# Attention 1: PE does the value products of two steps together in every second step

## The chip, the cores and the metric

The kernel runs on one core of a Trainium2 chip. The metric is the device time of one execution in microseconds (us), and the time shown is the median of several executions. PE is TensorE (PEld is its weight load), DVE is VectorE, ACT is ScalarE, POOL is GpSimd and SP is the queue that starts most DMAs.

## What is computed

The program is eight blocks in a row on an input of 2 x 1024 tokens with 128 features. The change touches only the first, a causal attention with 16 heads whose keys and values are made from a shared 32-wide latent. Cut to what matters, the reference is:

```
q      = einsum('bld,dhk->blhk', x, Wq)
latent = einsum('bld,dc->blc', x, Wkv_down)
k, v   = einsum('blc,chk->blhk', latent, Wk_up), einsum('blc,chk->blhk', latent, Wv_up)
attn   = softmax(where(causal, einsum('bqhd,bkhd->bhqk', q, k) / sqrt(64), -inf))
y      = einsum('bhqk,bkhd->bqhd', attn, v)
out    = einsum('bqhd,hdo->bqo', y, Wout)
```

The other seven blocks (a state-space layer, two spiking layers, two more attentions and two mixtures of experts) are written apart and are not changed.

## The kernel before

**Steps.** The attention is worked off in 96 steps, `STEPS` (t = 0 to 95). A group of four heads of one batch entry (`gg`, 8 of them) takes twelve steps: four for its first 512 queries (`c` = 0, key blocks `n` = 0 to 3) and eight for its last 512 (`c` = 1, `n` = 0 to 7). A step handles one block of 128 keys against up to 512 queries, for four heads. `width(t)` is how many queries are left under the causal mask: 512, 384, 256 and 128 for the last four blocks of either half. Below, the steps of one group are named by their numbers, and group 5, which is steps 60 to 71, stands for the others.

**What PE does in a step.** `scores(t, j)` is one matmul for each head (L532, plus the mask as a second matmul at L535 on diagonal blocks), in up to four slots that share three PSUM banks. A slot waits until ACT has taken the exponential (L695) of the slot three before it. `values(t)` multiplies the latent tokens with the exponentials of the four heads: four matmuls of 32 output columns (L548), each kept by the trace as two records, so eight records for one step. It needs all exponentials of step t. It writes bank 6 or 7. Below, V61 means `values(61)`.

**Items.** Between them PE works on a list of items, `PLAN[t]`, that prepares the next group: full score tiles for the row maxima (L581) and diagonal ones (L573 with the mask at L576), the projection of the queries (`mm3`, L46 to L48), the transposed maxima "n" (L587), the denominators "z" (L599, and L604 for late blocks) and, for a finished batch entry, the output projection "y" (L612). Items have three banks of their own. PE may begin item i only when DVE has worked off item i - 3 (the wait on `s0_af`); DVE needs one reduction for each score tile (L813, L825). An item "n" waits for the last maxima of DVE; its result goes through ACT (L711), DVE (L789) and a DMA before the scores of two steps later may start (`s0_nd`). An item "z" goes through ACT (L715, L716) and DVE (L794, L799).

**Order.** PE runs the program in the order in which it is written, and so do ACT, DVE and POOL. In step t it is: two score slots, the first third of the items, `values(t - 1)`, the second third, the other two score slots, the last third. So there is one value product in each step, one step behind its scores. POOL adds up the exponentials of the early blocks (L755); ACT may overwrite a tile of exponentials four steps later, once its value product is done (`s0_pv`) and POOL has added it (`s0_zp`). For the last half group (steps 88 to 95) PE makes the sums itself, right after the value products (L554).

Of the kernel before, what the change touches and what calls it, by code (L numbers as in the profile page):

```python
# [24 lines left out]
def wait(eng, sem, n):  # L25

    if n > 0:
        eng.wait_ge(sem, n)
# [26 lines left out]
def build(nc, a, out, upto=8):  # L55

    ctx = ExitStack()
    with ctx:
# [8 lines left out]
        def bank(i, n=1):  # L67
            return ps[:, i:i + n, :].rearrange("p b c -> p (b c)")
# [310 lines left out]
        N_STEP = len(STEPS)  # L379
        LAST = {2 * gg + c: 12 * gg + (3 if c == 0 else 11) for gg in range(NG0) for c in range(2)}  # L380

        def width(t):

            gg, c, n = STEPS[t]
            c0 = P * max(0, n - 4 * c)
            return c0, 512 - c0

        def slots(t):

            w = width(t)[1]  # L390
            return [(h, 1) for h in range(4)] if w > 256 else ([(0, 2), (2, 2)] if w == 256 else [(0, 4)])
# [51 lines left out]
        def parts(t):  # L443

            x = PLAN[t]
            if len(x) == 1 and x[0][0] == "n":
                return [], [], x
            k = (len(x) + 2) // 3
            return x[:k], x[k:2 * k], x[2 * k:]
# [35 lines left out]
        def s0_pe(pe):  # L485
# [37 lines left out]
            def scores(t, j):  # L523
                gg, c, n = STEPS[t]
                c0, w = width(t)
                h0, nh_ = slots(t)[j]
                e = SLOT_OF[t] + j
                if n == 0:
                    pe.wait_ge(s0_nd, 32 * (2 * gg + c + 1))
                wait(pe, s0_e, e - 2)  # L530
                o = bank(3 + e % 3)[:, 0:nh_ * w].rearrange("p (h q) -> p h q", h=nh_)
                ins = pe.matmul(o, kst[:, gg // G0, P * n:P * n + P], qst[gg % 2][:, c, h0:h0 + nh_, c0:512],  # L532
                                start=True, stop=True)
                if n >= 4 * c:
                    ins = pe.matmul(o[:, :, 0:P], ident_bf[:, :], causalT_bf.unsqueeze(1).to_broadcast([P, nh_, P]),  # L535
                                    start=False, stop=True, skip_group_check=True)
                ins.then_inc(s0_s, 1)

            def values(t):
                gg, c, n = STEPS[t]  # L540
                c0, w = width(t)
                u = 2 * gg + c
                src = zacc[u % 2] if n == 0 else pt[t % 4]
                pe.wait_ge(s0_e, SLOT_OF[t + 1])
                if n == 0:
                    wait(pe, s0_oc, u - 1)
                for h in range(4):
                    ins = pe.matmul(bank(6 + u % 2)[LD * h:LD * h + LD, c0:512], lat_tok[:, LB * (gg // G0) + n, :],  # L548
                                    src[:, h, 0:w], start=n == 0, stop=n == 4 * c + 3, skip_group_check=True)
                if (gg, c) == PE_SUMS:  # L550
                    i = AT[("z", u)]
                    wait(pe, s0_af, i - 2)
                    for h in range(4):
                        ins = pe.matmul(bank(i % 3)[LD * h:LD * h + LD, c0:512], ones32, src[:, h, 0:w],  # L554
                                        start=n == 0, stop=n == 4 * c + 3, skip_group_check=True)
                ins.then_inc(s0_pv, 1)
# [69 lines left out]
            for t in range(N_STEP + 2):  # L626
                first, second, third = parts(t)
                own = range(len(slots(t))) if t < N_STEP else []
                for j in own[:2]:
                    scores(t, j)  # L630
                for x in first:
                    item(x)
                if 0 < t <= N_STEP:
                    values(t - 1)
                for x in second:
                    item(x)
                for j in own[2:]:
                    scores(t, j)
                for x in third:
                    item(x)  # L640
# [2078 lines left out]
        def s6_dve(dve, link, s):  # L2719
# [40 lines left out]
            dve.reciprocal(w6i[:, (NTI - 1) % 2, :], z6[:, (NTI - 1) % 2, :]).then_inc(s6_wi_end, 1)  # L2760

        PE = {0: s0_pe, 1: s1_pe, 2: s2_pe, 3: s34_pe, 5: moe_pe, 6: s6_pe, 7: moe_pe}
        ACTS = {0: s0_act, 1: s1_act, 2: s2_act, 3: s34_act, 5: moe_act, 6: s6_act, 7: moe_act}
        DVE = {0: s0_dve, 1: s1_dve, 2: s2_dve, 3: s34_dve, 5: moe_dve, 6: s6_dve, 7: moe_dve}
# [99 lines left out]
```

## Time and profile before

| | |
|---|---|
| median of 3 runs | 2025.33 us (2019.01 to 2029.76) |
| the profiled execution | 2027.12 us, its span 2025.3 us |
| PE busy over the span | 1784.8 us, 88% |
| DVE, ACT, POOL busy | 79%, 59%, 47% |
| the 96 steps | about 67 to 434 us of the span |
| one group of 12 steps (V60 to V72) | 309.38 to 353.76 us, 44.38 us |

All numbers are times from the start of the profiled span or durations, in us unless ns is said. In rows of the timeline the first number is when a group of like instructions starts, the second how long it lasts in all, xN how many there are, and the bracket how long the engine had been idle and what ended that. The end of a matmul is modelled and its start is not, so distances between starts are read. A busy PE in this view is therefore not a PE at its peak.

### The profile page before, as it was taken

The page shows a single profiled execution, that of the slowest core. Times are in us where ns is not written, and L with a number is a line of the kernel's source. Part 1 is how long each engine was busy: PE and PEld are TensorE (multiplying, and loading weights), DVE is VectorE, ACT ScalarE, POOL GpSimd, SP SyncE. Part 2 cuts the span into 40 slices and gives each one's busy share as a digit, 9 for nine tenths or more (in the row PEclk, how much of TensorE's full clock was granted, in tenths as well). Part 3 has the DMA queues.
Part 4 walks back from the last instruction along what each step waited for, and adds up shares of the span by engine and source line. Part 5 has one row for each costly group of instructions (what it writes and reads, how often), then busy time and mean ns, then how long its engine had stood idle before and what let it go on. Part 6 is the DMA issues. An engine that isn't in the chain of part 4 may idle for free.

```text
span 2025.3 us, 33172 instructions
## 1 busy us (share of the span) xinstructions
PE 1784.8 (88%) x12499; PEld 1215.2 (60%) x12499; DVE 1596.5 (79%) x2099; ACT 1192.3 (59%) x2056; POOL 955.7 (47%) x386
## 2 busy tenths in 40 slices
PE   6899999887798987799999888889887777899999
PEld 5444454446455656677887555555555555678887
DVE  4566656528698988678876899999999999887777
ACT  2355444533697843446655667767777766655554
POOL 3266655612197951010000288878889889600000
PEclk9799999989799988799999999999999999999999
DMA  3111112000122220101100000000001000111000
GB/s 89 33 33 33 33 33 50 16 12 1 45 84 94 94 68 1 35 28 37 32 16 1 1 2 2 1 1 2 2 1 33 1 2 1 33 32 32 17 16 22
DMA packets 39555, 53.98 MB, mean 27 GB/s; under 512 B 6179, under 2 KB 22790, under 8 KB 39398
## 3 DMA queue, kind: packets, MB, share of 16 engines
q1 hardware_dynamic: 38870, 50.82, 9.0%
q8 instruction: 101, 1.65, 0.3%
q10 hardware_dynamic: 528, 1.05, 0.2%
q14 instruction: 56, 0.46, 0.1%
HBM read 37.83 MB, written 1.18 MB: 19 GB/s over the span
## 4 chain that ended last, share of the span: by engine, by line
PE 54%; issue 18%; DVE 18%; POOL 5%; ACT 3%; DMA 1%; SPq 0%; DVEq 0%; ACTq 0%; POOLq 0%; PEldq 0%
PE ps L46 10%; PE ps L47 9%; PE ps L48 9%; DVE negm L2724 7%; PE ps L1697 3%; PE ps L532 3%; PE ps L548 3%; PE ps L581 2%; PE ps L573 2%; DVE AF L2731 2%; PE ps L1685 2%; PE ps L2636 1%; POOL AR_plain L2529 1%; PE ps L2553 1%; DVE AF L825 1%
## 5 line engine op out<-in xcount | busy, mean ns | idle before, releaser
L2724 DVE TENSOR_REDUCE negm<-ps 128x64 bf16<-128x1024 f32 x256 | 301.8, 1213 | 20.1 <-PE ps L2627 20.0
L2529 POOL TENSOR_TENSOR AR_plain<-AF 128x2048 f32<-128x2048 f32 x64 | 261.7, 4094 | 31.5 <-ACT AF L2680 31.3
L46 PE MATMUL ps<-XH,AR 128*128 128x512 f32 x616 | 255.9, 415 | 23.4 <-DVE XL L251 5.9
L2688 ACT ACTIVATE AF<-ps 128x1024 f32<-128x1024 f32 x192 | 196.4, 1023 | 133.1 <-PE ps L2636 131.8
L755 POOL TENSOR_TENSOR AF<-AF 128x2048 f32<-128x2048 f32 (+3 forms) x52 | 184.7, 3551 | 179.1 <-ACT AF L695 176.2
L47 PE MATMUL ps<-XL,AR 128*128 128x512 f32 x616 | 245.5, 399 | 0.0
L48 PE MATMUL ps<-XH,AR 128*128 128x512 f32 x616 | 245.4, 398 | 0.0
L695 ACT ACTIVATE AF<-ps 128x512 f32<-128x512 f32 (+1 forms) x304 | 154.0, 576 | 147.4 <-PE ps L532 69.0
L2636 PE MATMUL ps<-negm,ident_bf 128*128 128x512 bf16 x512 | 161.3, 398 | 81.0 <-DVE negm L2724 80.6
L2731 DVE TENSOR_REDUCE AF<-AF 128x128 f32<-128x2048 f32 x96 | 218.4, 2275 | 0.0
L285 POOL TENSOR_SCALAR var_eps<-mv 128x8 f32<-128x8 f32 x10 | 4.2, 420 | 355.3 <-DVE mv L262 355.2
L1956 DVE TENSOR_TENSOR_SCAN AF<-AF,ps 128x1024 f32<-128x1024 f32 x64 | 144.4, 2275 | 18.4 <-PE ps L1685 12.8
L46 PEld LDWEIGHTS ps<-XH,AR 128*128 128x128 f32 x616 | 118.7, 193 | 66.7 <-issue 31.7
L2627 PE MATMUL ps<-AF_rounded,AR 128*128 128x256 f32 x704 | 149.5, 336 | 1.2 <-ACT AF L2688 1.1
L1335 ACT ACTIVATE AR_plain<-ps 128x512 f32<-128x512 f32 x128 | 76.5, 597 | 107.8 <-PE ps L48 107.8
L2529 POOL TENSOR_TENSOR hc<-AF 128x2048 f32<-128x2048 f32 x32 | 131.0, 4094 | 11.5 <-ACT AF L2680 11.5
L1377 DVE TENSOR_TENSOR AR_plain<-ps,AR_plain 128x512 f32<-128x512 f32 x128 | 88.1, 689 | 60.5 <-ACT AR_plain L1335 59.9
L48 PEld LDWEIGHTS ps<-XH,AR 128*128 128x128 f32 x616 | 118.9, 193 | 26.2
L47 PEld LDWEIGHTS ps<-XL,AR 128*128 128x128 f32 x616 | 119.3, 194 | 21.2
L2627 PEld LDWEIGHTS ps<-AF_rounded,AR 128*128 128x128 f32 x704 | 112.6, 198 | 31.3 <-ACT AF L2688 4.5
L2553 PE MATMUL ps<-AR_plain,AF 128*8 128x128 f32 x2752 | 113.7, 284 | 18.4 <-issue 12.3
L1335 ACT ACTIVATE AF<-ps 128x512 f32<-128x512 f32 x128 | 76.3, 596 | 87.7 <-PE ps L48 84.5
(329 smaller groups left out, 4199.2 us busy)
## 6 DMA issues: line engine op xcount, KB each, us to landing
AF<-scan_c_rows SPq DMA_DIRECT2D x32, 512.0 KB, 3.7
AR<-AR SPq DMA_DIRECT2D x96, 128.0 KB, 2.4
AF<-in_L_ffn_Wg_dram SPq DMA_DIRECT2D x21, 256.0 KB, 2.7
AF<-in_L_ffn_Wu_dram SPq DMA_DIRECT2D x21, 256.0 KB, 3.1
AF<-in_L_ffn_Wd_dram SPq DMA_DIRECT2D x21, 256.0 KB, 3.8
AF<-in_L_attn_a_Wq_dram SPq DMA_DIRECT2D x1, 512.0 KB, 4.0
AF<-in_L_attn_a_Wout_dram SPq DMA_DIRECT2D x1, 512.0 KB, 8.9
lnt<-in_L_ffn_W_fc_dram SPq DMA_DIRECT2D x2, 256.0 KB, 6.9
```

The source lines that it names most:

```text
L46: pe.matmul(out, ah, bh, start=start, stop=False)
L47: pe.matmul(out, ah, bl, start=False, stop=False)
L48: return pe.matmul(out, al, bh, start=False, stop=stop)
L695: act.activation(dst[:, h0:h0 + nh_, 0:w], bank(3 + e % 3)[:, 0:nh_ * w].rearrange("p (h q) -> p h q", h=nh_), ACT.Exp).then_inc(s0_e, 1)
L755: pool.tensor_tensor(zacc[u % 2][:, :, c0:512], zacc[u % 2][:, :, c0:512], pt[t % 4][:, :, 0:w], ALU.add).then_inc(s0_zp, 1)
L1335: act.activation(MSG[k][m % 3], bank(m % 2), ACT.Silu).then_inc(m_sg, 1)
L2529: pool.tensor_tensor(p6[m % 3].rearrange("p (j q i) -> p j q i", j=HJ, i=2), e6[m % 4].rearrange("p (j q i) -> p j q i", j=HJ, i=2), w6i[: ...
L2627: ins = pe.matmul(bank(2 * (j % 3) + x // 2)[:, 256 * (x % 2):256 * (x % 2) + 256], k6[g // LB][:, x, P * kb:P * kb + P], q[:, :, q0:q0 + ...
L2636: ins = pe.matmul(bank(2 * (j % 3) + h).rearrange("p (j q i) -> p j q i", j=4, i=2), ident_bf[:, :], negm6[:, j % 4, :].unsqueeze(1).unsqu ...
L2688: act.activation(o[:, :, q0:q0 + 2 * SUB], bank(2 * (j % 3), 2).rearrange("p (j c) -> p j c", j=HJ), ACT.Exp).then_inc(s6_e, 1)
L2724: dve.tensor_reduce(negm6[:, j % 4, :], bank(2 * (j % 3), 2).rearrange("p (j q i) -> p q j i", j=HJ, i=2), mybir.AxisListType.XY, ALU.max, ...
L2731: dve.tensor_reduce(z6[:, m % 2, :], e6[m % 4].rearrange("p (j q i) -> p q j i", j=HJ, i=2), mybir.AxisListType.XY, ALU.add).then_inc(s6_z ...
```

## The change

`values(t - 1)` is no longer run in each step. In an odd step (from 3 to 95) PE runs `values(t - 2)` and then `values(t - 1)`, where it ran `values(t - 1)` alone; in an even step it runs none. Steps 1 and 96 keep one each. So V1, V3, V5, ... V93 each move one step back, to stand just ahead of V2, V4, ... V94: 47 moves. Nothing is added or left out, and no other engine has a new instruction.

```diff
                 for x in first:
                     item(x)
-                if 0 < t <= N_STEP:
+                if t % 2 and 2 < t < N_STEP:
+                    values(t - 2)
+                if t == N_STEP or t % 2 and t < N_STEP:
                     values(t - 1)
                 for x in second:
                     item(x)
```

Three places show what it does to PE's order. First, PE in steps 62 and 63, before; the 32-wide L548 with 384 columns is V61, that with 256 is V62, and L587 is the item "n":

```order
L535 MATMUL ps<-AF,ident_bf 128x2x128
L548 MATMUL ps<-AF 32x384 x4
L587 MATMUL ps<-ident,AF 16x128
L532 MATMUL ps<-AR 128x512
L535 MATMUL ps<-AF,ident_bf 128x512
L573 MATMUL ps<-AR 128x128 x4
L576 MATMUL ps<-causal_bf,ident_bf 128x512
L573 MATMUL ps<-AR 128x256 x2
L576 MATMUL ps<-causal_bf,ident_bf 128x2x128
L548 MATMUL ps<-AF 32x256 x4
L573 MATMUL ps<-AR 128x256 x2
```

The same place on PE in the changed kernel:

```order
L535 MATMUL ps<-AF,ident_bf 128x2x128
L587 MATMUL ps<-ident,AF 16x128
L532 MATMUL ps<-AR 128x512
L535 MATMUL ps<-AF,ident_bf 128x512
L573 MATMUL ps<-AR 128x128 x4
L576 MATMUL ps<-causal_bf,ident_bf 128x512
L573 MATMUL ps<-AR 128x256 x2
L576 MATMUL ps<-causal_bf,ident_bf 128x2x128
L548 MATMUL ps<-AF 32x384 x4
L548 MATMUL ps<-AF 32x256 x4
L573 MATMUL ps<-AR 128x256 x2
```

V61 stood ahead of "n" and now stands behind it, next to V62. Second, PE in step 68, before, around V67 (L548), with score slots (L532, L535) and full tiles (L581):

```order
L581 MATMUL ps<-AR 128x512
L548 MATMUL ps<-AF 32x512 x4
L581 MATMUL ps<-AR 128x512
L532 MATMUL ps<-AR 128x512
L535 MATMUL ps<-AF,ident_bf 128x128
L532 MATMUL ps<-AR 128x512
L535 MATMUL ps<-AF,ident_bf 128x128
L581 MATMUL ps<-AR 128x512
```

The same place on PE in the changed kernel:

```order
L581 MATMUL ps<-AR 128x512 x2
L532 MATMUL ps<-AR 128x512
L535 MATMUL ps<-AF,ident_bf 128x128
L532 MATMUL ps<-AR 128x512
L535 MATMUL ps<-AF,ident_bf 128x128
L581 MATMUL ps<-AR 128x512
```

V67 is gone from between the tiles, and the next L548 is one of eight, V67 and V68, in step 69. Third, PE in step 70 around V69, as the difference from before (-) to after (+); L46 and L47 begin the projection of the next queries:

```order
-L581 MATMUL ps<-AR 128x512 x2
-L548 MATMUL ps<-AF 32x384 x4
-L581 MATMUL ps<-AR 128x512 x2
+L581 MATMUL ps<-AR 128x512 x4
 L46 MATMUL ps<-XH,AR 128x512
 L47 MATMUL ps<-XL,AR 128x512
```

V69 goes to step 71, and four full tiles, which share three banks, now follow one another directly.

## Rows read from the trace of the kernel before

**Rows 1.** Busy time by stretch: length, PE, PEld, DVE, ACT, POOL, clock, DMA.

```profile
200.00:250.00 50.00, 47.69 (x317) 24.26 (x315) 32.76 (x55) 25.50 (x51) 33.24 (x11) 1.00 0.16 33
```

**Rows 2.** Timeline of PE around V28: start, length, engine, line, operation, count.

```profile
190.50 0.40 PE L581 MATMUL ps<-AR 96*128 96x512 f32 x1
190.83 1.07 PE L548 MATMUL ps<-AF 128*32 128x512 f32 x8
191.82 0.50 PE L581 MATMUL ps<-AR 96*128 96x512 f32 x1
192.17 0.63 PE L532 MATMUL ps<-AR 128*128 128x512 f32 x2
```

**Rows 3.** Timeline of PE where two blocks of 32-column products adjoin (step 89).

```profile
414.57 1.06 PE L548 MATMUL ps<-AF 128*32 128x512 f32 x8
415.45 1.04 PE L554 MATMUL ps<-AF 128*32 128x512 f32 x8
416.43 0.96 PE L532 MATMUL ps<-AR 128*128 128x512 f32 x3
417.61 0.49 PE L532 MATMUL ps<-AR 128*128 128x512 f32 x1 [0.22 <-ACT AF L695]
```

**Rows 4.** Timeline of PE and DVE of PE in steps 62 to 64: the item n, V62, the next scores.

```profile
314.20 0.38 PE L587 MATMUL ps<-ident,AF 128*16 128x128 f32 x2 [0.58 <-DVE AF L833]
316.17 0.64 PE L548 MATMUL ps<-AF 128*32 128x256 f32 x8
317.74 0.30 PEld L532 LDWEIGHTS ps<-AR 128*128 128x128 f32 x2 [0.26 <-DMA AR<-AR]
```

**Rows 5.** Timeline in steps 64 to 66: V63, z's way through DVE, the item n.

```profile
318.94 0.42 PE L548 MATMUL ps<-AF 128*32 128x128 f32 x8
319.30 0.44 PE L573 MATMUL ps<-AR 96*128 96x384 f32 x1
324.01 0.69 DVE L794 SCALAR_TENSOR_TENSOR AF<-ps,AF 128x512 f32<-128x512 f32 x1 [3.00 <-ACT AF L716]
325.34 1.88 DVE L825 TENSOR_REDUCE AF<-ps 128x1 f32<-128x512 f32 x3
327.42 0.27 PE L587 MATMUL ps<-ident,AF 128*16 128x128 f32 x1 [0.62 <-DVEq L829]
```

**Rows 6.** Timeline in steps 67 to 69: V66, V67, V68.

```profile
331.68 0.50 PE L581 MATMUL ps<-AR 96*128 96x512 f32 x1
332.45 2.06 ACT L695 ACTIVATE AF<-ps 128x512 f32<-128x512 f32 x4 [1.03 <-PE ps L532]
333.89 1.06 PE L548 MATMUL ps<-AF 128*32 128x512 f32 x8
338.34 0.73 PE L581 MATMUL ps<-AR 96*128 96x512 f32 x2
```

**Rows 7.** Timeline in steps 69 to 72: V69, the query projections, V70, and DVE.

```profile
340.80 1.29 DVE L813 TENSOR_REDUCE AF<-ps 128x1 f32<-128x512 f32 x2 [0.63 <-PE ps L581]
342.27 0.40 PE L46 MATMUL ps<-XH,AR 128*128 128x512 f32 x1
344.42 2.96 DVE L825 TENSOR_REDUCE AF<-ps 128x4 f32<-128x512 f32 x5
345.09 0.51 PE L573 MATMUL ps<-AR 96*128 96x256 f32 x2
346.51 0.50 PE L46 MATMUL ps<-XH,AR 128*128 128x512 f32 x1 [0.23 <-DVE AF L825]
```

**Rows 8.** Busy time by short stretch in steps 2 and 3, columns as in rows 1.

```profile
79.60:80.45 0.85, 0.52 (x3) 0.32 (x3) 0.18 (x1) 0.10 (x1) 0.85 (x1) 0.95 0.00 0
80.45:81.30 0.85, 0.85 (x2) 0.15 (x1) 0.28 (x1) 0.16 (x1) 0.32 (x1) 0.50 0.00 0
...
86.40:87.25 0.85, 0.85 (x10) 0.38 (x10) 0.85 (x2) 0.00 (x0) 0.00 (x0) 0.53 0.00 0
```

**Rows 9.** Timeline of PE at the item n of step 2, ahead of that fall.

```profile
79.93 0.38 PE L587 MATMUL ps<-ident,AF 128*16 128x128 f32 x2 [1.57 <-DVE AF L833]
```

## The prediction, made before the changed kernel was run

> **What bounds the kernel now.** I read the busy time by stretch first, then the timeline of one whole group of steps. Over the steady part of the attention PE is busy for 47.69 of 50 us, DVE for 32.76, ACT for 25.50, POOL for 33.24, at full granted clock [rows 1]. So PE sets the pace on average, but its list is threaded through two others: each score slot waits for an exponential three slots back, each item for a DVE reduction three items back. The timeline shows three kinds of stretch. In steps 66 to 69 PE is nearly dense. Around each "n" PE waits for DVE: 0.58 us at the one and 0.62 us at the other [rows 4, 5]. Around steps 70 and 71 DVE is the fuller engine: five reductions take 2.96 us without a break, and PE waits for one of them [rows 7]. What a shorter PE list is worth has to be read in each of these stretches.
>
> **What joining two value products can save.** In a dense stretch a full-size matmul of 512 columns starts 0.23 to 0.24 us after the one before it. Around V28 the distances are: 0.33 us from the last L581 to the product, 0.99 us from the product to the next L581, and 0.35 us from there to the L532 [rows 2]. Where two blocks of 32-column products adjoin, the first takes 0.88 us instead of 0.99 (414.57 to 415.45) [rows 3]. So one way into such a block and out of it costs (0.33 - 0.23) + (0.99 - 0.88) + (0.35 - 0.23) = 0.33 us, and a pair pays it once instead of twice. With 47 pairs that is 15.5 us at the very most, if PE were the bound at each place. No instruction is added or dropped, so there is no other gain on PE.
>
> **Stretch by stretch, for steps 59 to 72**, with all times against those of before; minus is earlier.
>
> Steps 62 to 64. V61 (384 columns; 0.88 x 3/4 = 0.66 us as a second block of a pair) leaves a place where PE then waited 0.58 us for DVE anyway. DVE gets to the reduction ahead of "n" only after the two steps of "z" that come through ACT, so "n" stays at 314.20, and the removal gives nothing there; V59's move to step 61 is hidden by the same chain. Behind "n" V61 is in the way: of its 0.66 us the wait for the DMA of 0.26 [rows 4] swallows a part, and about +0.35 is left at the scores of step 64. What is queued behind it on PE is just those scores, and ACT waits for them.
>
> Step 64. V63 (128 columns) leaves. It took 0.36 us to its next matmul (318.94 to 319.30) [rows 5] and, by the 0.10 of V28, as much to enter; with the DVE reductions in time this gives -0.45. The slots behind it wait for ACT as before (0.22 us in the like place of rows 3). Together z starts at +0.35 - 0.45 = -0.1.
>
> Steps 65 and 66. V63 now adds 0.22 us (a quarter of 0.88) between z and V64. It is hidden: DVE is bound by z's way through ACT to 324.01, then three reductions of 1.88 us, then "n" at 327.42 [rows 5]. The second DVE operation of z needs V63, which is then long done. 0.
>
> Steps 66 and 67. V65 stood right behind "n", which has 16 output columns. Its removal gives 0.85 us, and as first block of the pair it costs 0.88. PE runs more slots in a row without a value product between them; ACT needs 2.06 us for four [rows 6], so the fourth slot waits a little longer than before. I get the tile after V66 at 331.58 instead of 331.68 [rows 6]: -0.1.
>
> Steps 67 to 69. V67 goes from 333.89 to stand ahead of V68. Eight slots now follow with no value product between them. ACT begins 0.43 us after the first slot, at 332.45, and takes 0.515 us for each; slot k may start 0.13 us after exponential k - 3. That puts slots 5 to 8 at 333.9, 334.3, 334.9 and 335.2, the last two tiles at 335.5 and 335.75, V67 at 336.1 and the tile after V68 at 337.95 instead of 338.34 [rows 6]: -0.4. This is the one stretch in which a whole 0.33 us and a little more comes through.
>
> Steps 69 to 71. V69 leaves from between four full tiles. There are three banks for them, and DVE takes 1.29 us for two [rows 7]. Without V69 the last tiles and the projection at 342.27 wait for DVE; the projection comes at 342.2. So V69's place gave PE work while it had to wait, and its removal is worth nearly nothing. But in step 71 V69 stands in front of V70 and adds 0.66 us before the tile at 345.09, whose reduction holds the next projection at 346.51 [rows 7]. DVE, which had been without a break there, now has a hole. I get the projection at 347.03: +0.5.
>
> Step 72. V71 (128 columns) leaves; the tile after it still waits for DVE to be done with the projection. -0.1 at z.
>
> The sum of a group is -0.1 (steps 62 to 64) - 0.1 (66, 67) - 0.4 (67 to 69) + 0.5 (69 to 71) - 0.1 (72) = -0.2 us of 44.38. I take it for seven groups: -1.4 us. In the last group there are no items to wait for; there PE and ACT alternate, with 1.18 us from the first slot to the fourth and a wait of 0.22 us for ACT [rows 3]. Eight slots in a row are bound by ACT (0.43 + 6 x 0.515 = 3.5 us until the second value product may start), then come two products and two sums (3 x 0.88 + 0.98 = 3.6 us): 7.2 us for two steps against 2 x 3.53 = 7.06. Three such pairs: +0.4. The whole: -1.0 us. Against the profiled execution of 2027.12 that is 2026.1; the median of the runs is 1.8 lower, so 2025.33 - 1.0 = **2024.3 us**. Each of the hand-made meetings above is uncertain by 0.2 to 0.3 us; if all five lean the same way, a group is off by about 1 us, and the sum by 7.
>
> POOL and the buffers: POOL's sum of the first block waits for the value product of an even step, which stays in its step behind one more product; it starts up to 0.9 us later. Nobody waits for POOL in these steps in the list of waits, and the tiles of exponentials have four steps of room, of which the odd ones lose one. 0. No DMA is moved in SP's queue.
>
> **Rivals.**
>
> Full gain: the waits that I put in place of V61, V67 and V69 don't come, and 0.31 to 0.33 us is gained for each pair: 47 x 0.31 = 14.6 us, 2010.8. Half of it is 2018, still within 0.5%. For it: PE's 47.69 of 50 us. Against it: the waits in rows 4, 5 and 7, in which DVE is what ends.
>
> The granted clock falls, slower: without V61 the hole of PE ahead of "n" grows from 0.58 to about 1.25 us, in each group. In step 2 a hole of 1.57 us [rows 9] stands just ahead of a fall of the granted clock from 1.00 to 0.50, which lasts from about 80.4 to 87.2 us [rows 8]. The stretch of rows 1, which holds a wait like that of 0.62 us [rows 5], stayed at 1.00. 6.8 us at half speed, with PE busy for 5.7 of them, cost up to 2.9 us, of which a wait for the DMA swallows 0.26: 2.6. Eight groups: +21 us, 2046; in half of them +10, 2035.7. It decides by whether the new hole of 1.25 us does what that of 1.57 did. For it: the two are near each other. Against it: PE is dense on both sides of the new hole, and no row shows the clock falling after so short a one.
>
> Starving of ACT and DVE, slower: in each pair PE gives nothing to either for 1.87 us instead of 0.99, with three banks each, that is 1.5 us of work for ACT. If each even step waits as step 70 does, the +0.5 of that stretch stands for -0.4 and -0.1 too: +0.9 a group, with the others about +1.2, over eight groups 10 us: 2035.
>
> The change does nothing that it says: excluded, since PE's order shows the eight L548 in one run.
>
> **How the numbers follow.** The forecast near no change, 2024.3, range of its own 2017 to 2032: 0.56. Full or most of the gain: 0.18, below 2015. Clock: 0.15. Starving: 0.11. What a measurement of this kernel can tell from no change is about 0.5%, 10 us: below 2015.2 counts as faster (0.18), above 2035.5 as slower: 0.15 + 0.11 less the cases that end inside, 0.22. That leaves 0.60. The range has to reach into both: 2011 takes in the full gain, and 2040 the starving and the clock's fall in half of the groups; the fall in all (2046) is left out.
>
> **What would show it.** Right: the group of 12 steps stays at 44 us; the tile after V68 comes 0.4 us earlier against V66's; the projection of step 71 later against it by 0.5; PE's idle time goes up while its switches go down; the wait ahead of "n" is 1.2 us. Wrong, to the fast side: a group of 42.5 us. To the slow side: granted clock of 0.50 after a "n" in steps 14 to 86, or new waits of PE for L695 of over 1 us in even steps.

## The result

| | median, us | executions |
|---|---|---|
| before | 2025.01 (2019.01 to 2030.83) | 16 |
| changed | 2032.64 (2028.06 to 2040.40) | 16 |

The ratio is 1.0036, with a 95% interval of 1.0024 to 1.0048: the change makes the kernel slower by 0.36%, about 7 us. That is under the 0.5% named in the prediction, but clear of zero. The forecast of 2024.3 was wrong; the range of 2011 to 2040 holds the time. The profiled execution of the changed kernel, one of the longer of the 16, took 2036.35 us, its span 2034.5. In the changed kernel all line numbers from 636 on are two higher: L548, L573, L581 and L587 are as before, L695 has become L697.

The busy time by stretch, the same 50 us as in [rows 1] (length, PE, PEld, DVE, ACT, POOL, clock, DMA):

```profile
200.00:250.00 50.00, 46.40 (x285) 24.04 (x284) 29.27 (x50) 24.63 (x50) 29.93 (x10) 0.93 0.15 33
```

Every engine did less in it, and the granted clock, 1.00 before, is 0.93. Finer slices, around the item n of step 38:

```profile
217.60:220.80 3.20, 1.84 (x7) 0.81 (x7) 2.03 (x5) 1.54 (x4) 2.82 (x1) 0.81 0.72 152
220.80:224.00 3.20, 3.20 (x18) 2.23 (x21) 1.36 (x2) 0.60 (x1) 3.06 (x3) 0.50 0.03 5
224.00:227.20 3.20, 3.20 (x20) 1.57 (x12) 0.71 (x2) 0.07 (x1) 2.36 (x2) 0.62 0.00 0
```

The clock is at its lower level, 1.2 GHz, for nearly 7 us. The timeline of PE in the changed kernel around it (step 38 is to its group what step 62 is in [rows 4]):

```profile
217.92 0.28 PE L535 MATMUL ps<-AF,ident_bf 128*128 128x256 bf16 x1
219.56 0.59 PE L587 MATMUL ps<-ident,AF 128*16 128x128 f32 x2 [1.36 <-DVE AF L835]
220.08 0.80 PE L532 MATMUL ps<-AR 128*128 128x512 f32 x1
223.12 2.36 PE L548 MATMUL ps<-AF 128*32 128x384 f32 x16
```

With V37 moved away PE has a hole of 1.36 us ahead of n, where it waited for 0.58 before [rows 4]. The L532 just behind lasts 0.80 us instead of 0.50, and the pair of value products 2.36 instead of 1.28 in a group at full clock:

```profile
322.41 0.38 PE L587 MATMUL ps<-ident,AF 128*16 128x128 f32 x2 [1.36 <-DVE AF L835]
322.72 0.50 PE L532 MATMUL ps<-AR 128*128 128x512 f32 x1
324.38 1.28 PE L548 MATMUL ps<-AF 128*32 128x384 f32 x16
326.28 0.71 PE L532 MATMUL ps<-AR 128*128 128x512 f32 x2
```

The hole is the same there and the clock does not fall. From the n of one group's third step to the next one's it is 44.38 us before (314.20 to 358.58). In the changed kernel it is 44.72 us with no fall (322.41 to 367.13), and 47.77 and 47.83 with one (171.79 to 219.56 to 267.39). So a fall of this length, 6.8 us at 1.2 GHz, costs 3.1 us. This execution has four falls between 100 and 400 us, three of 6.8 us and one of 3.4; the one before has none there.

The attention ends (first transpose of the next block) at 444.5 us before and at 449.5 after: 5.0 of the 9.2 us between the two profiled spans. From the n of step 14 to the n of step 86 the changed kernel takes 284.15 us instead of 272.73, 11.4 us more. But it had reached the n of step 14 3.6 us earlier (125.23 against 128.81): it was 1.8 us ahead at the n of step 2 already, and has no fall behind it as in [rows 8]; and from the n of step 86 to the end it takes 2.8 us less (40.2 against 43.0), partly because the execution before has one more fall there, at 438.8 us.

### The profile page after: what moved, and what is told of

Same layout as the page of the kernel before. It is cut to its first block, busy times and chain, and to the rows that moved or that the text cites. A ratio compares the mean times of both kernels' runs of the same rounds, so it can differ in the third digit from the quotient of the medians.

```text
span 2034.5 us, 33172 instructions
## 1 busy us (share of the span) xinstructions
PE 1789.1 (88%) x12499; PEld 1225.1 (60%) x12499; DVE 1591.1 (78%) x2099; ACT 1191.9 (59%) x2056; POOL 955.8 (47%) x386
## 4 chain that ended last, share of the span: by engine, by line
PE 57%; issue 18%; DVE 17%; POOL 5%; ACT 3%; DMA 1%; DVEq 0%; SPq 0%; ACTq 0%; POOLq 0%; PEldq 0%
PE ps L46 10%; PE ps L47 9%; PE ps L48 9%; DVE negm L2726 6%; PE ps L1699 3%; PE ps L532 3%; PE ps L548 3%; PE ps L573 2%; PE ps L2555 2%; PE ps L2638 2%; PE ps L581 2%; PE ps L1687 2%; POOL AR_plain L2531 2%; DVE AF L2733 1%; DVE AF L827 1%
## 5 line engine op out<-in xcount | busy, mean ns | idle before, releaser
L46 PE MATMUL ps<-XH,AR 128*128 128x512 f32 x616 | 257.5, 418 | 23.5 <-DVE XL L251 6.0
L47 PE MATMUL ps<-XL,AR 128*128 128x512 f32 x616 | 246.7, 401 | 0.0
L697 ACT ACTIVATE AF<-ps 128x512 f32<-128x512 f32 (+1 forms) x304 | 153.7, 577 | 149.9 <-PE ps L532 77.1
L46 PEld LDWEIGHTS ps<-XH,AR 128*128 128x128 f32 x616 | 119.5, 194 | 68.3 <-issue 31.6
L47 PEld LDWEIGHTS ps<-XL,AR 128*128 128x128 f32 x616 | 119.8, 195 | 21.3
L827 DVE TENSOR_REDUCE AF<-ps 128x1 f32<-128x384 f32 (+3 forms) x176 | 102.9, 636 | 33.3 <-PE ps L576 32.7
```

The costliest lines, as they stand in the source:

```text
L46: pe.matmul(out, ah, bh, start=start, stop=False)
L47: pe.matmul(out, ah, bl, start=False, stop=False)
L697: act.activation(dst[:, h0:h0 + nh_, 0:w], bank(3 + e % 3)[:, 0:nh_ * w].rearrange("p (h q) -> p h q", h=nh_), ACT.Exp).then_inc(s0_e, 1)
```

## Experiments

All of them change only where PE runs `values` or what it does while it waits. In the sources of the experiments `moved(t)` says which value products run one step later; the changed kernel has `t % 2 == 1 and t < 95`.

```diff
-                if 0 < t <= N_STEP:
+                if t >= 2 and moved(t - 2):
+                    values(t - 2)
+                if 0 < t <= N_STEP and not moved(t - 1):
                     values(t - 1)
```

### Keep V61 and its like in their own step

```diff
             def moved(t):
-                return t % 2 == 1 and t < N_STEP - 1
+                return t % 2 == 1 and t < N_STEP - 1 and t % 12 != 1
```

> As the changed kernel, but V1, V13, V25, ... V85 (the value product ahead of the item n in the third step of a group) stay in their own step; the other 39 moves are made. Theory A (the changed kernel is slower because PE's hole of 1.36 us ahead of n lets the granted clock fall to 0.50 in four groups, 3.1 us each): the hole is back at 0.6 us, no group from step 13 to 84 shows a granted clock under 1.00, a group takes 44.3 to 44.5 us, the time is 2024 to 2026. Theory B (the joined products starve DVE and ACT everywhere, and the clock adds little): 2030 or more.

Measured: 2026.73 us (12 executions, just above the 2024 to 2026 of theory A) against 2027.21 for the kernel before in the same series, ratio 0.9998 (0.9985 to 1.0012). The busy time by stretch over the group steps:

```profile
100.00:200.00 100.00, 93.59 (x613) 47.27 (x610) 62.12 (x106) 50.29 (x101) 62.15 (x21) 1.00 0.15 33
200.00:300.00 100.00, 94.11 (x631) 51.81 (x630) 59.77 (x103) 47.85 (x97) 62.66 (x20) 1.00 0.16 33
300.00:400.00 100.00, 94.77 (x660) 49.10 (x658) 61.59 (x105) 50.84 (x103) 55.54 (x18) 1.00 0.16 33
```

From 101 to 400 us there is no fall, the holes are of 0.58 us, and a group takes 44.38 to 44.68 us (the first 45.50; 45.53 in the kernel before). From the n of step 14 to that of step 86 it is 272.4 us. One fall stands just ahead of these stretches, at 97.4 us: moving V5 has widened the hole ahead of the n of step 6 from 0.93 us to 1.41. With 39 of the 47 joinings still made the loss is gone, so it does not come from joined products as such. Theory A stands and theory B falls. But there is no gain either, which has to be explained apart.

### Move V61 and its like alone

```diff
             def moved(t):
-                return t % 2 == 1 and t < N_STEP - 1
+                return t % 12 == 1
```

> As the kernel before, but V1, V13, ... V85 alone are moved one step back, behind the item n; no other product is moved. Theory A: the hole ahead of n is 1.2 to 1.4 us, the granted clock falls in about half of the groups at 3.1 us each, and in each group the scores of the fifth step come 0.33 us later: 2025.0 + 8 x 0.33 + 4 x 3.1 = 2040, less if the fall in step 2 of the kernel before (3 us) goes away: 2032 to 2040. Theory B: only the 0.33 us a group, 2027.6.

Measured: 2027.46 us median, but from 2021.91 to 2039.63; ratio 1.0016 (0.9997 to 1.0036), which settles no sign. The profiled execution is one of the long ones, 2035.69 us:

```profile
100.00:200.00 100.00, 94.05 (x605) 46.90 (x606) 62.71 (x105) 51.17 (x103) 62.86 (x21) 0.98 0.15 33
200.00:300.00 100.00, 94.00 (x607) 50.56 (x608) 56.80 (x97) 45.30 (x91) 56.95 (x20) 0.95 0.16 33
300.00:400.00 100.00, 93.87 (x586) 47.44 (x585) 60.28 (x100) 47.22 (x95) 56.86 (x19) 0.93 0.15 33
```

It has five falls between 100 and 400 us, so the hole alone is enough for falls. But the median lies under the 2032 to 2040 of theory A; it is the 2027.6 of theory B, which had no falls. The 12 executions stand apart in two lots, and the mean granted clock goes with them: seven of 2021.91 to 2027.54 us at 0.951 to 0.954, and five of 2031.69 to 2039.63 us at 0.948 to 0.950. So the long ones are those with the lower clock, and the median falls among the short ones. To count falls in another execution, the same kernel was profiled once more.

> The same kernel as e2_only61, whose times spread from 2021.9 to 2039.6; its profiled execution took 2035.7 us, with the granted clock down in six of the groups' holes. Theory A: an execution with another time has another number of falls, about 3 us for each. A profiled execution near 2025 to 2028 shows at most two falls more than the kernel before. If it shows as many falls as the other at a time 8 us shorter, the falls are not what costs.

Measured: 2026.38 us, and two short falls in these stretches instead of five:

```profile
100.00:200.00 100.00, 93.24 (x600) 46.36 (x598) 62.25 (x104) 50.70 (x102) 61.82 (x21) 0.98 0.16 33
200.00:300.00 100.00, 94.12 (x640) 50.61 (x636) 60.15 (x103) 47.90 (x96) 61.82 (x20) 1.00 0.16 33
300.00:400.00 100.00, 93.70 (x621) 47.96 (x617) 64.12 (x108) 48.70 (x97) 57.69 (x19) 0.98 0.16 33
```

The same program with the same holes ends its attention at 446.5 us here and at 453.1 with five falls: 6.6 of the 9.3 us between the two. From the n of step 14 to that of step 86 it takes 277.9 us here and 286.0 there. Why the median of this kernel lies 5 us under that of the changed one, with the same holes ahead of n, is not settled.

### Fill the hole

```diff
+                    if c:
+                        pe.wait_ge(s0_e, SLOT_OF[12 * gg + 2])
+                        for h in range(4):
+                            pe.matmul(o[LD * h:LD * h + LD, 0:384], lat_tok[:, 0, :],
+                                      pt[(12 * gg + 1) % 4][:, h, 0:384], start=True, stop=True,
+                                      skip_group_check=True)
                     pe.wait_ge(s0_m, u + 1)
```

The added matmuls go ahead of that wait in item n; their result is overwritten.

> The changed kernel, plus four matmuls of 32 output columns and 384 columns (the work of V1, V13, ... over again, into the item's own bank, where n then overwrites it) ahead of the wait of the item n, where V61 and its like stood before. PE has 0.7 us more work in each group. Theory A: the hole is 0.6 us, the granted clock stays at 1.00 in the groups, and though work was added the time falls from 2032.6 by about 12 us, to 2019 to 2024. Theory B: no change or slower, 2032 to 2034.

Measured: 2025.40 us, 7.2 less than the changed kernel (from another series), ratio to the kernel before 0.9997 (0.9985 to 1.0009). PE's timeline around the n of step 38, where L592 is the filling and L596 the n:

```profile
215.93 0.85 PE L592 MATMUL ps<-AF 128*32 128x384 f32 x8
217.26 0.39 PE L596 MATMUL ps<-ident,AF 128*16 128x128 f32 x2 [0.48 <-DVE AF L844]
217.59 0.50 PE L532 MATMUL ps<-AR 128*128 128x512 f32 x1
```

and the stretches:

```profile
100.00:200.00 100.00, 94.06 (x620) 48.10 (x618) 62.65 (x106) 51.78 (x104) 61.24 (x21) 1.00 0.16 33
200.00:300.00 100.00, 94.91 (x650) 52.27 (x653) 59.39 (x103) 47.16 (x94) 60.61 (x20) 1.00 0.16 33
300.00:400.00 100.00, 95.11 (x668) 48.84 (x660) 60.79 (x105) 50.49 (x102) 55.69 (x19) 1.00 0.16 33
```

All 47 joinings are there, PE has more work, and the time is not to be told from that of the kernel before. Between 100 and 400 us there is no fall. A group still takes 44.62 us, with 44.38 before: what the changed order costs without falls goes on; only the falls are gone. Theory A holds in kind. Its size, 12 us, was too large: 2025.40 us lies above its 2019 to 2024. From the n of step 14 to that of step 86 this execution takes 274.4 us, and the four profiled executions of the changed kernel (see the table below) 281.7 on average. So the falls of these steps cost about 7.2 us in an average execution.

With half as many columns:

> As e3_fill, with half the columns (192): the hole ahead of n in the third step of a group is 1.0 us instead of 0.5. Tells what the granted clock does after a hole between 0.6 us (no fall seen) and 1.36 us (falls in four of seven groups). If it still falls at times, 2025 to 2030; if not, 2024 to 2026, as e3_fill.

The edit is 192 for 384 in both places. Measured: 2025.87 us, spread from 2018.38 to 2033.12, ratio 1.0006 (0.9989 to 1.0022). The one profile has holes of 0.81 us and no fall between 68 and 443 us, but it is of the fastest of the 12 executions. The spread goes with the granted clock here too: its mean is 0.957 to 0.959 in the three fastest and 0.949 in the slowest (0.954 in the one next to it). Whether these falls stand behind the holes of 0.81 us or elsewhere, one profile can't say.

### Keep V69 too

```diff
             def moved(t):
-                return t % 2 == 1 and t < N_STEP - 1 and t % 12 != 1
+                return t % 2 == 1 and t < N_STEP - 1 and t % 12 not in (1, 9)
```

> As e1_keep61, but V9, V21, ... V93 (the product among four full score tiles) stay in their own step too. By the stretches of the changed kernel's trace V69 behind the projection costs 0.6 us a group, of which seven groups have it: 4 us less than e1_keep61, 2020 to 2022, if the two are independent. If the 0.6 us were hidden by a wait further on, the same time as e1_keep61.

Measured: 2022.31 us, ratio to the kernel before 0.9971 (0.9956 to 0.9985), and 4.4 us less than with V69 moved. Three of its groups take 43.73 to 43.84 us. In its timeline the products V67 and V68 are joined, V69 stands alone, and the two projections come as long after V68 as before:

```profile
333.18 1.92 PE L548 MATMUL ps<-AF 128*32 128x512 f32 x16
337.62 0.85 PE L548 MATMUL ps<-AF 128*32 128x384 f32 x8
338.97 0.40 PE L46 MATMUL ps<-XH,AR 128*128 128x512 f32 x1
341.23 0.64 PE L548 MATMUL ps<-AF 128*32 128x256 f32 x8
343.21 0.50 PE L46 MATMUL ps<-XH,AR 128*128 128x512 f32 x1 [0.23 <-DVE AF L830]
```

From V67 to the second projection it is 10.03 us; in the changed kernel it is 10.63 (344.48 to 355.11). So the 0.6 us is V69's.

### Join in one dense place only

```diff
             def moved(t):
-                return t % 2 == 1 and t < N_STEP - 1
+                return t % 12 == 7 and t < 84
```

> As the kernel before, but only V7, V19, ... V79 are joined with the product of the next step, seven moves in the one stretch where PE is dense. By the stretch (the tile after V68 0.33 us earlier against V66's) 7 x 0.33 = 2.3 us less than the kernel before, 2024.9; if the gain is taken back at the next wait for DVE, no change, 2027.2.

Measured: 2026.55 us, ratio 0.9992 (0.9977 to 1.0008): not to be told from no change. In the trace the group takes 44.02 us against 44.38, in four groups alike. So the gain of one joining, 0.36 us, is there and reaches the end of the group; 2.5 us in all is less than the executions differ.

### Fill the waits that the kernel before had

Four matmuls of 512 columns, once or twice, are put where PE only waits: ahead of the n of steps 2 and 6 and ahead of the scores of steps 4 and 88. For this PE now waits for the exponential ahead of its wait for the queries, not behind it.

```diff
+            def fill(o, rounds):
+                for _ in range(rounds):
+                    for h in range(4):
+                        pe.matmul(o[LD * h:LD * h + LD, 0:512], lat_tok[:, 0, :],
+                                  lat_tok.rearrange("p t c -> p (t c)"), start=True, stop=True,
+                                  skip_group_check=True)
...
+                if j == 0 and t in (4, 88):
+                    fill(bank(3 + e % 3), 1 if t == 4 else 2)
...
+                    if (gg, c) in ((0, 1), (1, 0)):
+                        fill(o, 1)
```

> The kernel before, no product moved, plus the same filling matmuls as f1_best_fill. Its trace had falls at 80.4 us (2.6 us by the prediction) and 404.9 us. Theory A: both are gone, 2027.2 - 5 = 2021 to 2023. Theory B (a fall costs nothing off the DVE and DMA chains): 2026 to 2028.

Measured: 2022.07 us against 2025.81 in the same series, ratio 0.9989 (0.9976 to 1.0001). The median is where theory A had it, but the interval just holds 1, so a gain is not shown. The clock is at 1.00 where it had been 0.86 and 0.83 in the kernel before. The first two rows are the kernel before, the last two the filled one:

```profile
76.00:100.00 24.00, 19.62 (x104) 9.41 (x104) 11.80 (x22) 9.10 (x19) 10.49 (x5) 0.86 0.01 2
400.00:420.00 20.00, 17.12 (x101) 5.62 (x99) 3.01 (x6) 10.25 (x20) 9.50 (x5) 0.83 0.00 1
76.00:100.00 24.00, 21.69 (x142) 9.30 (x140) 12.98 (x25) 10.58 (x21) 12.22 (x5) 1.00 0.01 2
400.00:420.00 20.00, 18.16 (x124) 7.44 (x125) 1.82 (x4) 11.33 (x22) 8.30 (x5) 1.00 0.01 2
```

> e4_keep61_69 plus idle-filling matmuls of 32 output columns, four of 512 columns (0.9 us) at each of five points where PE only waits: ahead of the items n of steps 2 and 6, ahead of the scores of step 4, and twice ahead of those of step 88; their results are overwritten. If the granted clock's falls after such holes cost what the halved speed says (about 3 us each, two of them in e4_keep61_69's trace of the attention), 2022.3 - 5 = 2017 to 2018. If the falls are hidden by other waits, 2022 as e4_keep61_69.

Measured, with V61 and V69 and their like kept in their own step as above: 2018.87 us against 2025.81, ratio 0.9972 (0.9960 to 0.9984). The medians differ by 6.9 us, the ratio says 5.7. It has the lowest median of this study. But against the kernel before the same kernel without the fillings had a ratio of 0.9971, so the fillings are not shown to gain anything beyond it. In the profiles its attention ends at 436.7 us, against 439.9 without them.

### Is all of the loss in the attention?

In the two first profiles 4.2 of 9.2 us stand in blocks that the change does not touch. Both kernels were therefore profiled again.

> The changed kernel once more, for another execution's pattern of falls. Theory A: against the first (2036.35 us in all, four groups with a fall between 120 and 280 us) a time lower by 3 us for each fall fewer; groups without a fall take 44.7 us, with one 47.8.

> The kernel before, unchanged, for a second execution. In the first the attention ended at 444.5 us of the span (the first transpose of the next block) and the rest took 1580.8. If the rest varies by itself, by falls of the clock in other blocks, it lies between 1578 and 1586 as in the other kernels, whatever the attention does. If it is 1581 again in all executions of this kernel, the change makes the other blocks slower too.

> As i1_before, a third execution of the kernel before: the rest of the program between 1578 and 1586 us by chance, or 1581 each time.

> The changed kernel, a third execution. The attention ended at 449.5 and at 445.1 us in the first two, the rest took 1585.0 and 1586.0. By chance: a rest between 1578 and 1586. By the change: 1585 again.

> The changed kernel, a fourth execution: a rest between 1578 and 1586 us by chance, or 1585 again by the change; the attention's end later than in the kernel before by 0.4 to 0.45 us for each us that the granted clock is longer at 0.50.

The fourth column is the time from the n of step 14 to that of step 86, the last from the end of the attention to the last matmul of L2118 (L2120 in the changed kernel), in the blocks behind it.

| execution | span, us | attention ends | steps 14 to 86 | the rest | to L2118 |
|---|---|---|---|---|---|
| before, first | 2025.3 | 444.5 | 272.7 | 1580.8 | 441.1 |
| before, second | 2021.4 | 443.7 | 272.2 | 1577.7 | 440.6 |
| before, third | 2016.4 | 442.9 | 271.5 | 1573.5 | 441.1 |
| changed, first | 2034.5 | 449.5 | 284.2 | 1585.0 | 446.3 |
| changed, second | 2031.1 | 445.1 | 277.6 | 1586.0 | 446.5 |
| changed, third | 2030.4 | 449.0 | 280.7 | 1581.4 | 446.5 |
| changed, fourth | 2035.2 | 450.3 | 284.2 | 1584.9 | 446.1 |

The attention is longer by 4.8 us on average (448.5 against 443.7). Between steps 14 and 86 it is longer by 9.5 us; ahead of them and behind them the changed kernel is faster, by 3.1 and 1.7 us. The changed executions have four, two, three and four groups with a fall between 105 and 400 us, those of the kernel before none, and the one with two falls is the one that ends at 445.1. Steps 14 to 86 grow with the time at 1.2 GHz in these groups: 277.6, 280.7 and 284.2 us for 6.8, 13.7 and 23.9 us, or 0.38 us for each us (0.4 to 0.45 had been expected). Groups with a short fall (3.4 us) take 46.3 to 46.6 us, those with a long one (6.8 us) 47.8 to 48.1. So the second execution, with two falls fewer than the first, is shorter by 4.4 us in its attention and not by the 6 expected: both of its falls are short.

Counted over all the profiled executions, between 100 and 400 us, for the n of a group's third step (a fall counts if it begins from 0.3 us ahead of n to 2.3 us behind it; there is no other between 105 and 400 us):

| hole ahead of n, us | holes | followed by a fall |
|---|---|---|
| 0.48 to 0.58 | 54 | 0 |
| 0.80 to 0.81 (one execution) | 6 | 0 |
| 1.35 to 1.36 | 36 | 20 |

Of the six groups between the n of step 14 and that of step 74 that have no fall and no output projection, in the four changed executions, four take 45.1 to 45.7 us instead of 44.7. In one of them (second execution, 45.12 us) the first diagonal tile behind n waits for the DMA of the projected queries, whose projection comes later than before:

```profile
220.51 0.63 PE L573 MATMUL ps<-AR 96*128 96x128 f32 x4 [0.20 <-DMA AR<-AR]
```

The rest is not 1585 each time, nor 1581: it goes from 1573.5 to 1580.8 before and from 1581.4 to 1586.0 in the changed kernel. In the other kernels it is anywhere from 1578.1 to 1585.0, and it is not tied to how long the attention takes: with V67 and its like alone joined the attention ends at 439.2 us, 4.5 us early, and the rest takes 1584.9, so that the whole is no faster. But all four of the changed kernel lie above all three of the one before, by 7.0 us on average. The last column places 5.4 us of this within the next blocks. There the time goes with where the granted clock falls. In each of the 16 profiled executions one fall begins 38.3 to 39.8 us behind the end of the attention. Where it begins at 38.5 to 39.4 (all three of the kernel before, and five others), L2118 is reached after 440.6 to 441.6 us; where it begins at 39.6 to 39.8 (all four of the changed kernel, and two others), after 446.1 to 446.5; in the two with 38.3 and 38.4, after 444.8. This is seen and not tested by an experiment, and why the changed kernel was on the late side four times is open.

The seven profiled spans differ by 11.8 us on average, 4.8 in the attention and 7.0 in the rest; the medians of the result differ by 7.6. So the profiled executions can't share out the difference of the medians. What the experiments show is that without the holes it is gone.

## Why the prediction was wrong

**The step that failed** is the first term of the sum, steps 62 to 64, where it was said of V61's leaving that "the removal gives nothing there". The time of n was taken to stay, and the granted clock behind it too. What the runs show in its place is the second rival, "The granted clock falls, slower", which was given 0.15 and left out of the forecast: a hole of 1.36 us (1.25 forecast), a fall in two to four of the six groups whose n lies between 100 and 400 us, and with them about 7.2 us in steps 14 to 86. The argument against it, that PE is dense on both sides of the hole, carried nothing. Its price was set too low for one long fall, 2.6 us for 3.1, and its number too high, eight places, or four in its milder form, for two to four of which some are short. Filling the hole and leaving V61 in its place each take the loss away. That the range holds the time is owed to its having been stretched to 2040 for this rival and for the starving one.

**What joining can save.** The 0.33 us a joining was right: 0.36 us where PE is dense, measured alone.

**Steps 62 to 64** were forecast at -0.1 and came at +0.1: from n to z it is 7.50 us (322.41 to 329.91) instead of 7.38. V61 behind n delays the scores of step 64 by 0.33 us, as forecast with 0.35. V63's removal gives 0.2 us and not 0.45, and DVE, which is "in time" in the prediction, runs six reductions there without a break (326.26 to 329.41 us) behind a wait of 0.84 us for PE. That the diagonal tiles of step 64 then wait for it is read from the small gaps between them; no run tests it.

```profile
326.26 3.15 DVE L827 TENSOR_REDUCE AF<-ps 128x2 f32<-128x512 f32 x6 [0.84 <-PE ps L576]
```

**Steps 65 and 66**, forecast at 0: from z to n it is 5.84 us in both.

**Steps 66 to 69.** From n to the tile after V66 it is 4.26 us in both kernels, with -0.1 forecast; to the tile after V68, 10.59 instead of 10.92: -0.33, with -0.4 forecast for it.

```profile
335.75 0.38 PE L587 MATMUL ps<-ident,AF 128*16 128x128 f32 x2 [0.62 <-DVEq L831]
340.01 0.50 PE L581 MATMUL ps<-AR 96*128 96x512 f32 x1
344.48 1.92 PE L548 MATMUL ps<-AF 128*32 128x512 f32 x16
346.34 0.73 PE L581 MATMUL ps<-AR 96*128 96x512 f32 x2
```

**Steps 69 to 71** were forecast at +0.5 and came at +0.6. The four full tiles now meet DVE and wait, where V69 had stood before, and the second projection is late:

```profile
348.79 2.48 DVE L815 TENSOR_REDUCE AF<-ps 128x1 f32<-128x512 f32 x4 [0.63 <-PE ps L581]
349.54 0.50 PE L581 MATMUL ps<-AR 96*128 96x512 f32 x1 [0.33 <-DVE AF L815]
350.13 0.50 PE L46 MATMUL ps<-XH,AR 128*128 128x512 f32 x1
355.11 0.50 PE L46 MATMUL ps<-XH,AR 128*128 128x512 f32 x1 [0.23 <-DVE AF L827]
```

That is 8.77 us from the tile after V68 to the projection, instead of 8.17 [rows 6, 7].

**Step 72**, forecast at -0.1: from the second projection to the next n it is 12.02 us instead of 12.07 (to 367.13 and to 358.58).

**The last group** was forecast at +0.4. The two blocks of that sum, 3.5 and 3.6 us, make 7.1 and not 7.2, which leaves +0.2. It came out on the other side: from the first scores of step 88 to V95 it is 26.35 us in the changed kernel (409.41 to 435.76, second execution) and 27.26 in the one before (407.10 to 434.36, second execution), each with a fall of 3.4 us.

**The sum of a group** is +0.34 us (44.72 against 44.38) where -0.2 was forecast. The signs of the two large terms, steps 67 to 69 and 69 to 71, were right, and without the falls the forecast of "no change" holds: with the hole filled the kernel is at 0.9997. The full gain, the first rival, did not come for the reason given against it: around n and in steps 69 to 71 DVE is what ends the waits. The starving rival is not seen: with 39 joinings left and no falls nothing is lost.

The Trainium skill, page "TensorEngine Tiling (Array Packing)", section "Key Properties", says that changing the tiling mode drains the engine; the 0.36 us gained where only V67 and its like are joined agrees with it.

## What to carry to other kernels

Work that stands in front of a wait may be worth more than the time it takes: it costs little there, and it keeps the engine from standing still. Here 0.66 us of it, moved behind the wait, brought falls that cost about 7 us in the changed kernel. Before moving it, look for the holes that it would leave, and compare them with those behind which the granted clock fell in the same trace. Join where the engine is dense and leave alone what fills a wait: 39 joinings without V61 gave nothing, and leaving out V69's too gave 0.3%. And do not read a gain in one block from the whole time alone: the blocks behind it took 5 us more or less here, with the place at which the clock fell in them.

## What was not expected of the hardware

The same program has the granted clock fall in other groups from one execution to the next, after holes of the same 1.36 us; the two executions of the kernel with V61 alone moved had five and two falls and ended their attention at 453.1 and 446.5 us. A hole of 1.53 us ahead of the n of step 2 had no fall behind it in the first execution of the changed kernel, where one of 1.57 had [rows 9] and one of 1.54 had in the third execution:

```profile
78.10 0.38 PE L587 MATMUL ps<-ident,AF 128*16 128x128 f32 x2 [1.53 <-DVE AF L835]
```

Nor is a shorter hole safe. Ahead of the n of step 6 the kernel before has one of 0.93 us, and in its second execution the granted clock was at 0.50 from 100.8 us on. Of the six profiled executions with this hole it is the only one with such a fall; of the eight in which V5 is moved and the hole is 1.40 us, four have one:

```profile
99.05 0.38 PE L587 MATMUL ps<-ident,AF 128*16 128x128 f32 x2 [0.93 <-DVEq L829]
100.80:104.20 3.40, 3.40 (x12) 0.99 (x12) 1.29 (x2) 1.16 (x3) 3.14 (x1) 0.50 0.03 5
```

And matmuls that compute nothing of use, put where PE waits, undid a loss: 2025.40 us with the holes of the changed kernel filled, where it took 2032.64 without. That they make a kernel faster that had no such loss is not shown: 0.9989 (0.9976 to 1.0001) in the kernel before.
